# Four attention layers on one core: the row fills split in halves and moved, and two of six operand copies issued by GpSimd

## Chip, cores and metric

The kernel runs on one core of a Trainium2 chip. The metric is the device time of one execution in microseconds; where several runs are given it is their median. Engines are named TensorE (PE), VectorE (DVE), ScalarE (ACT), GpSimd (POOL) and SyncE (SP). PEld is the weight load of TensorE, which runs beside its matmuls.

## The reference, cut to what matters

Sixteen sequences `x` of 128 tokens and 128 channels pass through four layers with a context of the same shape. Layer L3 has a self and a cross attention, so there are five attention parts. A part does, for each sequence:

```python
# L0: layernorm of both inputs, 8 heads of 16 channels; all others 16 heads of 8 channels
q, k, v = x @ Wq + bq, ctx @ Wk + bk, ctx @ Wv + bv      # L3 self: all three from x
scores = einsum('bhqd,bhkd->bhqk', q, k) / sqrt(d)        # L1: causal and padding mask; L3 self: the same
probs = softmax(scores)
x = x + einsum('bhqk,bhkd->bhqd', probs, v)               # L2, L3: also @ Wo + bo
# L2: then x += gelu(x @ W1 + b1) @ W2 + b2
# L3 self: layernorm; L3 cross: layernorm, the same kind of MLP, layernorm
```

Everything is float32 in and out.

## The kernel before, in words

The 16 sequences are taken in 8 sets of two. A *unit* is one set in one of the five parts (L0, L1, L2, L3S, L3C), so there are 40 units, numbered `u` = 8 x part + set. `SETS` is 8, `RING` is 4.

**The split.** Scores are made by bf16 matmuls whose contraction rows carry the float32 product in pieces. For a unit, TensorE projects q and k (`qk`, L978 and L979), ScalarE adds the bias into `qk_f32` (L642), then ScalarE writes the first bf16 term (`split`, L654, signal `split1_done`). For units from 2 on GpSimd makes the remainder (`rest`, L560), the second term (`term1`, L562, `split2_done`) and the third (`term2`, L568, `split_done`). For units 0 and 1 VectorE does this (L777, L780, L785).

**The stacks.** The list `PRODUCTS` has six pairs of terms, (0,0), (0,1), (1,0), (1,1), (0,2), (2,0). For each one DMA (`stack` step `c` = 0 to 5, L442) spreads the two terms from the 128 channel partitions into rows of an operand tile, one row per channel of a head and 16 heads (8 in L0) side by side: 128 KB in pieces of 512 bytes. The tile is `pairs8` in L0 and one half (64 rows) of `pairs16` later: units `u` and `u+4` share it. All six are issued by SP. Stacks 4 and 5 use the third term, so SP waits for `split_done` before stack 4; before stack 0 it waits until the last attention matmul of unit `u-4` has read the tile. The readers of the stacks are the first score matmul of the unit on TensorE (L930, through `stacked`), and ScalarE's `split` of unit `u+2`, which overwrites the terms that the stacks read.

**The rows behind the stacks.** Below its 48 product rows a half of `pairs16` has 4 mask rows and 3 rows for the negated maxima. They start as constants: `fill_rows(pool, r)` (L385) copies 7 rows of `template` to 16 heads of half `r`, 112 KB. The sources and the targets are seven partitions. Halves 0 and 1 are filled ahead of GpSimd's steps, 2 and 3 at its step `ln_in` of unit 0. `mask_rows` (L397) then writes a unit's mask rows, 32 KB. L0 has its own tiles, whose 3 rows ScalarE fills at the start (L610).

**Softmax.** VectorE takes the maxima of the scores (L823), splits them (`nmax`, L833, L836), TensorE transposes them (`n_tr`, L995), VectorE copies them (L839), and SP writes them with a DMA into the tile (L458). Then TensorE makes the scores a second time, transposed and with the maxima taken off (`attn`, L1016), ScalarE exponentiates them (L703), TensorE multiplies with v (`pv`, L1043). From L1 on the scores of unit `u+1` run interleaved with the attention matmuls of unit `u`.

**The order.** It is fixed ahead: `schedule()` gives every step a position of 8 per unit (`PREPARE`, `STACK_AT`, `SCORE_AT`, `CHAIN`, `LAST`) and sorts them into `STEPS`. Each of the five engines walks the same list and does its own part of each step, in order, so a wait on an engine holds up all its later steps. The order of some steps around the change, as the list gives it (numbers are units, the dots stack numbers):

```
L0  ln_in 0, ln_in 1, ln_in 2, stack 0.4, 0.5, qk 1, ln_in 3, score 0, qk 2, stack 1.4, 1.5, rest 2
L0  term2 5, ln_in 7, mask 0, stack 5.4, 5.5, rest 6, term1 6, term2 6, mask 1, stack 6.4, 6.5, rest 7
L1  rest 15, term1 15, term2 15, rest 16, term1 16, term2 16, stack 15.4, 15.5, qk 17
L2  rest 17, term1 17, stack 16.4, term2 17, stack 16.5, qk 18, rest 18, term1 18, stack 17.4, term2 18, stack 17.5
L3C rest 33, stack 32.4, term1 33, term2 33, stack 32.5
```

GpSimd has more at some of these steps: `ln_in` makes the reciprocal deviations (L531, L534), at unit 2 four small loads (L547 to L550), at unit 4 a weight load; `mask` makes the mask rows of L1 (L495, L498) and, for units 0 to 3, writes them (L397) after waiting for all four fills; `term2` has a weight load (L577) in L1 and L2, and mask rows (L397) for units 12 to 19, 24 to 27 and 32 to 35. SP issues the loads of `x_tok` and `c_tok` for all sets first (L407, L409).

Of the kernel before, what the change touches and what calls it, by code (L numbers as in the profile page):

```python
# [50 lines left out]
MISC_BANKS = 3  # L51
SLOT = 8
SPLIT_BY_DVE = 2
EPS_LN, EPS_LAST = 1e-5, 1e-6
# [161 lines left out]
def build(nc, x, ctx_in, weights, cols, rows, valid, valid_t, pad, pad_t, out):  # L216
    with ExitStack() as stack:
# [3 lines left out]
        def sem(name):  # L221
            return stack.enter_context(nc.semaphore(name))
# [67 lines left out]
        tokens_landed = [sem(f"tokens_landed{s}") for s in range(SETS)]  # L290
        stack_landed = [sem(f"stack_landed{r}") for r in range(RING)]
        max_landed = [sem(f"max_landed{r}") for r in range(4)]
        out_landed = sem("out_landed")
# [10 lines left out]
        mask_landed = [sem(f"mask_landed{r}") for r in range(RING)]  # L304
        fill16_landed = sem("fill16_landed")
        misc_ready = sem("misc_ready")
# [66 lines left out]
        def stacked(eng, u):  # L373

            eng.wait_ge(stack_landed[u % RING], (u // RING + 1) * 16 * len(PRODUCTS))

# [3 lines left out]

        def fill_rows(pool, r):

            first = product_rows(SETS)
            rows_ = slice(HALF * (r % 2) + first, HALF * (r % 2) + first + MASK_ROWS + TERMS)
            pool.dma_start(pairs16[r // 2][rows_, :, :, :].rearrange("p h a n -> p h (a n)"),  # L385
                           template[first:first + MASK_ROWS + TERMS, :, :, :].rearrange("p a b n -> p (a b n)")
                           .unsqueeze(1).to_broadcast([MASK_ROWS + TERMS, 16, 2 * TOK])).then_inc(fill16_landed, 16)

        def mask_rows(pool, u):

            part = u // SETS
            tile, base = stack_of(u)
            source = {L1: mask_rows_l1[:, PAIR * (u % SETS):PAIR * (u % SETS + 1), :],
                      L2: zero_rows[:, :].rearrange("p (b n) -> p b n", b=PAIR),
                      L3S: mask_rows_l3s[:, :, :], L3C: mask_rows_l3c[:, :, :]}[part]
            first_row = base + product_rows(u)
            pool.dma_start(tile[first_row:first_row + MASK_ROWS, :, 1, :],  # L397
                         source.rearrange("p b n -> p (b n)").unsqueeze(1)
                         .to_broadcast([MASK_ROWS, HEADS[part], TOK])).then_inc(mask_landed[u % RING], 16)

        block = stack.enter_context(nc.Block())

        @block.sync
        def _(sp):
# [10 lines left out]
            for step in STEPS:  # L415
                u = step.u
                part = u // SETS
                heads = HEADS[part]
                if step.kind == "stack":

                    c = step.b
                    tile, base = stack_of(u)

                    if c == 0:
                        sp.wait_ge(split1_done, u + 1)
                    if c == 1:
                        sp.wait_ge(split2_done, u + 1)
                    if c == 4:
                        sp.wait_ge(split_done, u + 1)
                    if c == 0:  # L430
                        if u >= RING and (u - RING) // SETS >= min(part, L1):

                            freed = the("attn", u - RING, PAIR - 1, heads // QUAD - 1)
                            sp.wait_ge(attn_ready, NUM[freed] + 1)
                        if u == SETS:
                            sp.wait_ge(fill16_landed, 16 * RING)
                    d = D // heads
                    tq, tk = PRODUCTS[c]
                    terms = terms_ring[u % 2]
                    gap = TERMS + tk - tq  # L440

                    sp.dma_start(tile[base + c:base + product_rows(u):len(PRODUCTS), :, :, :],  # L442
                                 terms[:, :, :, :].rearrange("p a t n -> p (a t) n")[:, tq:tq + gap + 1:gap, :])\
                        .then_inc(stack_landed[u % RING], 16)
                if step.kind == "store":
# [17 lines left out]
        def _(pool):  # L463
# [19 lines left out]
            pool.wait_ge(rows_ready, 3)  # L483
            fill_rows(pool, 0)
            fill_rows(pool, 1)
            for step in STEPS:
# [15 lines left out]
                if step.kind == "mask" and u < RING:  # L502

                    pool.wait_ge(fill16_landed, 16 * RING)
                    pool.wait_ge(mask_l1_ready, u + 1)
# [30 lines left out]
                if step.kind == "ln_in" and u == 0:  # L536
                    fill_rows(pool, 2)
                    fill_rows(pool, 3)
                    pool.memset(causal_t[:, :], 0.0).then_inc(negated_diagonal, 1)
# [24 lines left out]
                if step.kind == "term2" and u >= SPLIT_BY_DVE:  # L564
                    pool.wait_ge(split2_done, u + 1)
                    if 2 <= u < SETS:
                        pool.wait_ge(maxterms_ready, ub(the("nmax", u - 2, 1)) + 1)
                    pool.tensor_tensor(terms[:, :, 2, :], rest[:, :, :], terms[:, :, 1, :], ALU.subtract)\  # L568
                        .then_inc(split_done, 1)
                if step.kind == "term2" and part in W_EACH:  # L570

# [6 lines left out]
                if step.kind == "term2" and u in MASKED_ANEW and u >= SETS + RING:  # L578
# [5 lines left out]
                    if u == L3S * SETS:  # L584
                        pool.wait_ge(mask_l3_ready, 1)
                    mask_rows(pool, u)
                if step.kind == "square":
                    half = slice(2 * step.b, 2 * step.b + 2)
# [551 lines left out]
```

## Time and profile before

| | us |
|---|---|
| runs of the kernel | 496.58, 497.14, 505.9 |
| median | 497.14 |
| profiled execution, its own time | 495.54 |
| its span, first to last instruction | 493.8 |

The span is 1.74 us shorter than the execution's own time; that rest lies around the instructions. All times from the trace count from the start of the span. The page's busy shares are averages; the chain of waits follows the work that ended last back to its releasers.

### The profile page before, as it was taken

The page shows a single profiled execution, that of the slowest core. Times are in us where ns is not written, and L with a number is a line of the kernel's source. Part 1 is how long each engine was busy: PE and PEld are TensorE (multiplying, and loading weights), DVE is VectorE, ACT ScalarE, POOL GpSimd, SP SyncE. Part 2 cuts the span into 40 slices and gives each one's busy share as a digit, 9 for nine tenths or more (in the row PEclk, how much of TensorE's full clock was granted, in tenths as well). Part 3 has the DMA queues.
Part 4 walks back from the last instruction along what each step waited for, and adds up shares of the span by engine and source line. Part 5 has one row for each costly group of instructions (what it writes and reads, how often), then busy time and mean ns, then how long its engine had stood idle before and what let it go on. Part 6 is the DMA issues. An engine that isn't in the chain of part 4 may idle for free.

```text
span 493.8 us, 17187 instructions
## 1 busy us (share of the span) xinstructions
PE 447.9 (91%) x6720; PEld 302.8 (61%) x6720; DVE 386.2 (78%) x1099; ACT 321.9 (65%) x660; POOL 234.2 (47%) x290
## 2 busy tenths in 40 slices
PE   3478989899999998899999999999999999999981
PEld 2365656556666665577767666666666666666761
DVE  6587897778878878889988877888889987877552
ACT  2345765457676667678777676667677787777841
POOL 6246576856734534454554444334444543222345
PEclk9657998899999999999999999999999999999997
DMA  7644343643433444433433322222244341220001
GB/s 125 167 101 104 91 102 82 142 115 87 106 84 93 111 110 98 101 93 94 91 77 62 68 51 68 68 69 69 53 86 94 76 93 47 63 56 14 14 23 32
DMA packets 71579, 40.48 MB, mean 82 GB/s; under 512 B 7896, under 2 KB 70584, under 8 KB 71500
## 3 DMA queue, kind: packets, MB, share of 16 engines
q1 hardware_dynamic: 69280, 36.04, 30.2%
q0 software_dynamic: 2112, 3.24, 4.7%
q8 instruction: 55, 0.90, 0.8%
q14 instruction: 24, 0.20, 0.1%
q10 hardware_dynamic: 108, 0.10, 0.1%
HBM read 4.74 MB, written 1.05 MB: 12 GB/s over the span
## 4 chain that ended last, share of the span: by engine, by line
PE 76%; DVE 10%; DMA 4%; issue 3%; ACT 2%; POOL 2%; SPq 1%; POOLq 0%; DVEq 0%; ACTq 0%
PE attn_ps L1016 17%; PE o_ps L1043 15%; PE misc_ps L1073 6%; PE misc_ps L1064 5%; PE misc_ps L978 5%; PE misc_ps L1050 4%; PE score_ps L897 4%; PE misc_ps L984 3%; PE misc_ps L979 3%; DVE max_words L823 3%; PE misc_ps L1056 2%; DVE normed_in L759 2%; PE misc_ps L995 2%; DMA c_tok<-in_ctx_dram 2%; PE score_ps L930 2%
## 5 line engine op out<-in xcount | busy, mean ns | idle before, releaser
L823 DVE TENSOR_REDUCE max_words<-score_ps 128x4 f32<-128x512 f32 x288 | 193.7, 683 | 50.5 <-PE score_ps L930 47.6
L703 ACT ACTIVATE probs<-attn_ps 128x512 f32<-128x512 f32 x288 | 169.7, 601 | 74.4 <-PE attn_ps L1016 68.5
L1016 PE MATMUL attn_ps<-pairs 55*128 55x128 bf16 (+1 forms) x1152 | 113.7, 220 | 9.0 <-DMA pairs<-max_rows 3.4
L930 PE MATMUL score_ps<-pairs 52*128 52x128 bf16 (+1 forms) x1152 | 115.4, 222 | 2.3 <-DMA pairs<-terms 2.0
L560 POOL TENSOR_TENSOR rest<-qk_f,terms 128x512 f32<-128x512 f32 x38 | 44.2, 1162 | 114.2 <-ACT terms L654 114.2
L1016 PEld LDWEIGHTS attn_ps<-pairs 55*128 55x128 bf16 (+1 forms) x1152 | 64.9, 95 | 53.3 <-issue 26.8
L1043 PE MATMUL o_ps<-probs,v 128*32 128x128 f32 x2304 | 96.8, 281 | 0.1
L930 PEld LDWEIGHTS score_ps<-pairs 52*128 52x128 bf16 (+1 forms) x1152 | 67.3, 96 | 6.5 <-DMA pairs<-terms 2.8
L1043 PEld LDWEIGHTS o_ps<-probs,v 128*32 128x32 f32 x2304 | 53.5, 109 | 23.4 <-issue 9.5
L568 POOL TENSOR_TENSOR terms<-rest,terms 128x512 bf16<-128x512 f32 x38 | 44.0, 1158 | 9.7 <-DVE max_words L836 7.2
L712 ACT ACTIVATE o_sb<-o_ps 128x256 f32<-128x256 f32 x80 | 30.9, 386 | 23.7 <-PE o_ps L1043 22.7
L531 POOL TENSOR_SCALAR var_eps<-mean_var 128x2 f32<-128x2 f32 (+1 forms) x32 | 7.1, 222 | 81.1 <-DVE mean_var L744 80.8
L562 POOL TENSOR_TENSOR terms<-qk_f,terms 128x512 bf16<-128x512 f32 x38 | 43.9, 1154 | 0.0
L1050 PE MATMUL misc_ps<-ident,o_sb 128*128 128x128 f32 x160 | 35.0, 302 | 1.2 <-DVE attn_tok L859 1.2
L1073 PE MATMUL misc_ps<-hidden,w 128*128 128x256 f32 x128 | 33.3, 388 | 1.7 <-ACT hidden L691 1.6
L1064 PE MATMUL misc_ps<-xT,w 128*128 128x256 f32 x128 | 31.2, 386 | 0.3 <-DVE xT L881 0.3
L865 DVE SCALAR_TENSOR_TENSOR xT<-misc_ps,col,xT 128x256 f32<-128x256 f32 x40 | 19.0, 480 | 11.5 <-PE misc_ps L1073 6.6
L590 POOL TENSOR_TENSOR gelu_arg<-half_h 128x512 f32<-128x512 f32 x16 | 16.2, 1030 | 23.1 <-ACT half_h L688 23.1
L1073 PEld LDWEIGHTS misc_ps<-hidden,w 128*128 128x128 f32 x128 | 23.0, 190 | 6.4 <-ACT hidden L691 2.0
L534 POOL TENSOR_TENSOR rstd<-var_eps,minus_half 128x2 f32<-128x2 f32 (+1 forms) x32 | 25.6, 799 | 2.7
L654 ACT ACTIVATE terms<-qk_f 128x512 bf16<-128x512 f32 x40 | 25.3, 632 | 2.3 <-DMA pairs<-terms 1.7
L1064 PEld LDWEIGHTS misc_ps<-xT,w 128*128 128x128 f32 x128 | 23.0, 190 | 4.0 <-issue 0.8
(121 smaller groups left out, 751.0 us busy)
## 6 DMA issues: line engine op xcount, KB each, us to landing
pairs<-terms SPq DMA_DIRECT2D x240, 128.0 KB
x_tok<-in_x_dram SPq DMA_DIRECT2D x8, 128.0 KB, 2.6
c_tok<-in_ctx_dram SPq DMA_DIRECT2D x8, 128.0 KB, 3.0
pairs<-max_rows SPq DMA_DIRECT2D x64, 12.0 KB
w<-in_weights_dram POOLq DMA_DIRECT2D x8, 128.0 KB, 3.2
out_dram<-x_tok SPq DMA_DIRECT2D x8, 128.0 KB, 1.8
w<-in_weights_dram POOLq DMA_DIRECT2D x5, 192.0 KB, 3.3
pairs<-template POOLq DMA_DIRECT2D x4, 112.0 KB, 7.9
```

Source lines behind the costliest of these rows:

```text
L560: pool.tensor_tensor(rest[:, :, :], qk_f32[:, :, :], terms[:, :, 0, :], ALU.subtract)
L562: pool.tensor_tensor(terms[:, :, 1, :], qk_f32[:, :, :], terms[:, :, 0, :], ALU.subtract)\
L568: pool.tensor_tensor(terms[:, :, 2, :], rest[:, :, :], terms[:, :, 1, :], ALU.subtract)\
L703: act.activation(probs[n % PROBS_RING][:, :, :].rearrange("p h q -> p (h q)"), attn_ps[n % 2][:, :], ACT.Exp, scale=float(D // HEADS[part] ...
L712: act.activation(o_sb[n % 2][:, :], o_ps[:, 0:2 * P], ACT.Copy)\
L823: dve.tensor_reduce(max_words[ub(step) % 2][:, QUAD * g:QUAD * (g + 1)], score_ps[n % 2][:, :].rearrange("p (h k) -> p h k", h=QUAD), AX_X ...
L930: return pe.matmul(score_ps[NUM[step] % 2][:, j * S:(j + 1) * S], tile[score_rows(u), QUAD * g + j, 0, b * S:(b + 1) * S], tile[score_rows ...
L1016: last = pe.matmul(attn_ps[n % 2][:, j * S:(j + 1) * S], pairs[attn_rows(u), h, 1, b * S:(b + 1) * S], pairs[attn_rows(u), h, 0, b * S:(b ...
L1043: last = pe.matmul(o_ps[32 * j:32 * j + 32, region * P:(region + 1) * P], values, probs[n % PROBS_RING][:, j, :], start=part == L0 or g % ...
L1050: last = pe.transpose(bank[:, k * P:(k + 1) * P], o_sb[ub(step) % 2][:, k * P:(k + 1) * P], ident[:, :])
L1064: last = pe.matmul(bank[:, half * TOK:(half + 1) * TOK], weight(f"w1_{part}_{2 * b + half}"), xT[s][:, :], start=True, stop=True)
L1073: last = pe.matmul(bank[:, 0:TOK], weight(f"w2_{part}_{c}"), hidden[:, c, :], start=(c == 0), stop=(c == 3))
```

## The change

Three things are edited. `BY_POOL` is 4. The stacks with `c` of 4 and 5 are issued by GpSimd at the same places of the list, with a ring of signals of their own (`late_landed`); GpSimd waits before stack 4 for `split_done` of the unit and for the last attention matmul of unit `u-4`. SP keeps stacks 0 to 3 and their waits. The four fills become eight halves of 8 heads each (56 KB), and are issued by GpSimd right after `rest` and after `term2` of units 2 to 5, half `r` of `pairs16` at unit `r + 2`; their signal becomes one per half, and the mask step of unit `u` waits for its own half alone.

```diff
+BY_POOL = 4
+        late_landed = [sem(f"late_landed{r}") for r in range(RING)]
-        fill16_landed = sem("fill16_landed")
+        fill16_landed = [sem(f"fill16_landed{r}") for r in range(RING)]
         def stacked(eng, u):
-            eng.wait_ge(stack_landed[u % RING], (u // RING + 1) * 16 * len(PRODUCTS))
+            eng.wait_ge(stack_landed[u % RING], (u // RING + 1) * 16 * BY_POOL)
+            eng.wait_ge(late_landed[u % RING], (u // RING + 1) * 16 * (len(PRODUCTS) - BY_POOL))
-        def fill_rows(pool, r):
+        def fill_rows(pool, r, heads):
-            pool.dma_start(pairs16[r // 2][rows_, :, :, :].rearrange("p h a n -> p h (a n)"),
+            pool.dma_start(pairs16[r // 2][rows_, heads, :, :].rearrange("p h a n -> p h (a n)"),
...
-                           .unsqueeze(1).to_broadcast([MASK_ROWS + TERMS, 16, 2 * TOK])).then_inc(fill16_landed, 16)
+                           .unsqueeze(1).to_broadcast([MASK_ROWS + TERMS, 8, 2 * TOK])).then_inc(fill16_landed[r], 16)
+        def stack_rows(eng, u, c):
+            tile, base = stack_of(u)
+            tq, tk = PRODUCTS[c]
+            gap = TERMS + tk - tq
+            eng.dma_start(tile[base + c:base + product_rows(u):len(PRODUCTS), :, :, :],
+                          terms_ring[u % 2][:, :, :, :].rearrange("p a t n -> p (a t) n")[:, tq:tq + gap + 1:gap, :])\
+                .then_inc((stack_landed if c < BY_POOL else late_landed)[u % RING], 16)
...
-                if step.kind == "stack":
+                if step.kind == "stack" and step.b < BY_POOL:
...
-                    if c == 4:
-                        sp.wait_ge(split_done, u + 1)
...
-                        if u == SETS:
-                            sp.wait_ge(fill16_landed, 16 * RING)
...
+                    stack_rows(sp, u, c)
...
-            fill_rows(pool, 0)
-            fill_rows(pool, 1)
...
-                    pool.wait_ge(fill16_landed, 16 * RING)
+                    pool.wait_ge(fill16_landed[u], 32)
...
-                    fill_rows(pool, 2)
-                    fill_rows(pool, 3)
...
+                if step.kind in ("rest", "term2") and SPLIT_BY_DVE <= u < SPLIT_BY_DVE + RING:
+                    if u == SPLIT_BY_DVE:
+                        pool.wait_ge(rows_ready, 3)
+                    fill_rows(pool, u - SPLIT_BY_DVE, slice(0, 8) if step.kind == "rest" else slice(8, 16))
...
+                if step.kind == "stack" and step.b >= BY_POOL:
+                    if step.b == BY_POOL:
+                        pool.wait_ge(split_done, u + 1)
+                        if u >= RING and (u - RING) // SETS >= min(part, L1):
+                            freed = the("attn", u - RING, PAIR - 1, HEADS[part] // QUAD - 1)
+                            pool.wait_ge(attn_ready, NUM[freed] + 1)
+                    stack_rows(pool, u, step.b)
```

## Rows read from the trace of the kernel before

**Rows 1.** The page: busy time, and the span in 40 slices.

```profile
PE 447.9 (91%) x6720; PEld 302.8 (61%) x6720; DVE 386.2 (78%) x1099; ACT 321.9 (65%) x660; POOL 234.2 (47%) x290
...
PE   3478989899999998899999999999999999999981
```

**Rows 2.** Chain that ended last, to 70 us (start us, us, what).

```profile
3.74 11.50 DMA c_tok<-in_ctx_dram
...
32.03 2.81 DVE normed_in L759 x4
```

**Rows 3.** Timeline of the first 33 us (start us, us, engine line, tiles, idle before).

```profile
3.85 1.51 POOL L385 DMA_DIRECT2D pairs<-template  x2 [0.31 <-POOL template L480]
...
5.08 5.03 SPq L409 DMA_DIRECT2D c_tok<-in_ctx_dram  x1
...
15.26 0.49 DVE L740 BATCH_NORM_STATS2 stats<-x_tok 128x6 f32<-128x128 f32 x2 [4.51 <-DMA c_tok<-in_ctx_dram]
...
24.14 0.67 POOL L547 DMA_DIRECT2D validt_raw<-in_valid_t_dram  x1
24.22 0.61 DVE L759 TENSOR_SCALAR normed_in<-x_tok,mean_var,rstd 128x128 f32<-128x128 f32 x2 [1.47 <-POOL rstd L534]
...
28.08 0.61 PE L930 MATMUL score_ps<-pairs 96*128 96x128 bf16 x4 [0.66 <-DMA pairs<-terms]
...
32.17 1.21 POOL L560 TENSOR_TENSOR rest<-qk_f,terms 128x512 f32<-128x512 f32 x1 [0.19 <-ACT terms L654]
```

**Rows 4.** Windows: stretch, us, busy of PE, PEld, DVE, ACT, POOL, PE clock, DMA share, GB/s.

```profile
4.00:8.00 4.00, 1.03 (x4) 0.63 (x4) 2.47 (x13) 1.94 (x3) 3.69 (x6) 1.00 0.97 209
8.00:13.00 5.00, 3.47 (x11) 2.75 (x12) 2.40 (x8) 1.29 (x3) 1.12 (x5) 1.00 0.83 51
17.00:21.00 4.00, 1.08 (x4) 0.71 (x4) 2.85 (x9) 0.58 (x2) 1.00 (x1) 0.53 0.68 196
```

**Rows 5.** Issues of stacks and fills (ns min/median/max); then landing of L577, 155 to 200 us.

```profile
L442 SPq DMA_DIRECT2D pairs<-terms x240: 565/623/1970, 21.2 to 433.1; - x120
L385 POOL DMA_DIRECT2D pairs<-template x4: 618/661/861, 3.9 to 7.6; - x4
...
DMA to landing us min/median/max: 2.9/3.7/4.6
```

**Rows 6.** Landing of GpSimd's mask rows, L397, 155 to 200 us.

```profile
DMA to landing us min/median/max: 3.3/4.1/4.5
```

**Rows 7.** Timelines of POOL, SP and PE, 67 to 100 us.

```profile
67.09 1.09 POOL L495 TENSOR_SCALAR mask_rows_l<-valid_raw 4x256 bf16<-4x256 uint8 x1
67.42 2.68 SPq L442 DMA_DIRECT2D pairs<-terms  x4
70.38 1.16 POOL L560 TENSOR_TENSOR rest<-qk_f,terms 128x512 f32<-128x512 f32 x1
73.72 0.39 PE L930 MATMUL score_ps<-pairs 96*128 96x128 bf16 x4
...
85.96 1.17 POOL L560 TENSOR_TENSOR rest<-qk_f,terms 128x512 f32<-128x512 f32 x1
...
93.12 1.17 POOL L560 TENSOR_TENSOR rest<-qk_f,terms 128x512 f32<-128x512 f32 x1
```

**Rows 8.** Timelines of ACT and POOL, splits of units 17 to 20.

```profile
167.57 0.66 ACT L654 ACTIVATE terms<-qk_f 128x512 bf16<-128x512 f32 x1
...
168.31 1.15 POOL L560 TENSOR_TENSOR rest<-qk_f,terms 128x512 f32<-128x512 f32 x1 [4.95 <-ACT terms L654]
...
172.34 0.64 POOL L397 DMA_DIRECT2D pairs<-zero_rows  x1
...
177.41 0.66 ACT L654 ACTIVATE terms<-qk_f 128x512 bf16<-128x512 f32 x1
...
186.97 0.66 ACT L654 ACTIVATE terms<-qk_f 128x512 bf16<-128x512 f32 x1
...
196.04 0.62 ACT L654 ACTIVATE terms<-qk_f 128x512 bf16<-128x512 f32 x1
```

More of the change, by code:

```diff
@@ L418, in _ @@
                 heads = HEADS[part]
-                if step.kind == "stack":
+                if step.kind == "stack" and step.b < BY_POOL:
                     c = step.b
-                    tile, base = stack_of(u)
                     if c == 0:
@@ L434, in _ @@
                             sp.wait_ge(attn_ready, NUM[freed] + 1)
-                        if u == SETS:
-                            sp.wait_ge(fill16_landed, 16 * RING)
[L437 to L444, printed above, removed]
+                    stack_rows(sp, u, c)
                 if step.kind == "store":
```

## The prediction

> **What bounds the kernel now.** I read the page's busy times and slices first. TensorE is busy 447.9 of 493.8 us, and its slices are 8 or 9 tenths full from the fourth on, but 3, 4 and 7 in the first three [rows 1]. So in the middle an edit off TensorE pays nothing unless it makes TensorE wait, and a delay comes out one to one; at the start there are idle stretches to win. The chain of waits, read next for the start, shows one large item: from 3.74 on, 11.50 us go to the landing of the context tokens of set 1 [rows 2]. The timeline shows why that transfer is slow. GpSimd issues the first two fills at 3.85, and SP, busy with the token loads, is then held 5.03 us in one issue [rows 3]. In 4 to 8 us the DMA engines are 97% busy at 209 GB/s; in 8 to 13 us still 83%, but only 51 GB/s move; in 17 to 21 us, without fills, 196 GB/s at 68% [rows 4]. Engines that are busy and move little are waiting on something narrow. The fills read seven partitions and write seven, so I put the slow stretch down to them. Their replacement in time is what the change is about.
>
> After that I looked for where stacks decide, since two of six change their queue: the score of unit 0 waits for a stack landing, 0.66 us [rows 3]; and ScalarE's split of unit u+2 needs all stacks of unit u landed.
>
> **Part one: the fills leave the start.** VectorE idled 4.51 us before the statistics of set 1, for that landing [rows 3]. Without fills the tokens should land before VectorE is free, at 15.26 - 4.51 = 10.75 us. So the statistics, and the reciprocal deviations and normalising behind them, come 4.5 us earlier: that is the most this edit alone gives. What is late next is the score of unit 0. It needs stacks 4 and 5, which GpSimd now issues after `ln_in` of set 2 and the four small loads behind it. Those loads start at 24.14 and the last at 26.00 for 0.55 [rows 3]; moved by 4.5 they end at 22.05. Two issues of 0.65 follow, the second from 22.7. With a landing of 3.5 (an estimate, between the 2.9 and 3.7 of [rows 5]) it is there at 26.2. The score ran at 28.08, so there only 1.9 us are left of the 4.5. Then a side effect: VectorE's four `normed_in` of set 3 took 2.81 [rows 2], beside `rest` and `term1` of unit 2 on GpSimd from 32.17; two of them without such company took 0.61, so four 1.1 or a little more [rows 3]. Set 3's deviations come early while `rest` waits for the score, so the two separate: 1.7 more. Value taken: 1.9 + 1.7 = 3.6 gained. Ends: 1.9, and 4.5 + 1.7 = 6.2.
>
> A rule of the Trainium skill bears on the overlap: the page "Advanced Engine Details and Errata" says that the second VectorE port is shared with GpSimd, whose instructions and VectorE's two-port ones block each other. The 2.81 agrees. By "DMA: Bandwidth & Descriptors", section "SWDGE vs HWDGE vs iDMA", it would also hold GpSimd's descriptor writing, and so speak against the stacks' new place. Here the rows show no such price: the small load at 24.14 beside `normed_in` at 24.22 took 0.67, the last one 0.55 [rows 3].
>
> **Part two: the eight halves beside sets 2 to 5.** A fill's issue takes GpSimd 0.62 to 0.86, median 0.66 [rows 5]; a half has half the pieces, so I take 0.65. Eight are 5.2 us of GpSimd for 2.7 before. GpSimd is in front of nothing there except `term1` and the deviations, and in this stretch the chain goes through VectorE; cost taken, zero. Their 448 KB can hold up stacks as they held up tokens, but now in eight portions: zero to 2 us, taken 0, since the chain to 70 us has no stack landing on it in what I kept of it and each half is an eighth of the traffic.
>
> **Part three: 80 stack issues move from SP to GpSimd.** SP's issue takes 0.62 in the median [rows 5]; GpSimd's own issues of 32 to 128 KB take 0.55 to 0.86 [rows 3, 5]. No row shows GpSimd issuing 256 pieces of 512 bytes. Nearest in size is the 128 KB load; I take 0.65, and 1.3 (twice that) as the upper end; below 0.55 nothing speaks for it. Taking 1.25 us per unit from SP gives nothing where SP waits anyway; bounded from above by 1 us in all, taken 0.
>
> Where is GpSimd itself in front? Two places.
>
> (a) 67 to 100 us. From 85.96 to 93.12 it goes round without a gap in 7.16 us [rows 7], and two issues make that 8.5. First, unit 5: SP issued its last four stacks from 67.42 in 2.68, the last one at about 69.4, and the score ran at 73.72. GpSimd must finish mask step 0 first (from 67.09; `rest` of unit 6 followed at 70.38). With one fill before it, 0.65, and the first stack before the second, 0.65, the last is issued at 71.7, 2.3 later. The same landing and 73.72 make the score 2 us late, less what the last SP stack gains by a shorter queue. For units 6 to 9 GpSimd's lag grows by 1.3 each, but the units' spacing of 8 to 9 us takes that up. Taken: 1.5 lost. Ends: 0 and 3.
>
> (b) The entry to L2, units 15 to 19. Stack 5 of unit u now leaves behind `term2` of u+1, its weight load and its mask rows; split u+2 waits for its landing; and `rest` of u+2 waits for that split. That is a circle that the kernel before doesn't have. Its length by the rows: split 17 starts at 167.57, GpSimd's last item starts at 172.34 for 0.64, so 5.41; plus stack 4 inserted, 0.65: stack 5 is issued 6.06 after the split [rows 8]. Landing: 2.9 to 4.6 for a weight load, 3.3 to 4.5 for mask rows with a median of 4.1 [rows 5, 6]. With 4.1 the circle is 10.16. The splits stood 9.84, 9.56 and 9.07 apart [rows 8], so it is late by 0.32 + 0.60 + 1.09 = 2.0; unit 15, whose two stacks also leave behind unit 16, adds an estimated 0.5. From unit 20 on mask rows are missing and periods are longer. Taken: 2.5 lost, out of TensorE, which has no slack to give back. Ends: landing 2.9 makes 8.96, no loss; 4.6 makes 10.66, and 0.82 + 1.10 + 1.59 + 1.0 = 4.5.
>
> By the Trainium skill, "DMA: Bandwidth & Descriptors", section "Anatomy of one DMA — SWDGE (gpsimd) path", a GpSimd DMA takes about 2.0 us plus bytes over 436 GB/s, 2.3 for a stack. Then the circle would be 8.4 and (b) cost nothing, and the sum below would be 2.5 lower. GpSimd's DMAs here took 2.9 at the least [rows 5], so I go by the rows.
>
> In L3C stack 5 has the same place, behind `term2` of u+1 and mask rows. Before, it was the last of six from SP and equally late; taken 0, up to 1.
>
> **The sum.** -3.6 + 0 + 1.5 + 2.5 + 0 = +0.4 on the profiled execution of 495.54, so 495.9. That execution lay 1.6 under the median of the runs, 497.14, so the median to expect is 497.5.
>
> **The rivals.**
> - *The start alone counts.* The stacks land within 3.5 us and GpSimd's lag in 67 to 100 us is absorbed, so (a) and (b) are 0 or a small rest. For it: units lie 9 us apart and GpSimd is busy 234.2 of 493.8. Against it: the gapless stretch of [rows 7]. Price: -3.6 to -4.5, median 493.
> - *GpSimd's issue of a 256-piece stack is the price* (slower). Each takes 1.3 us where 0.65 is taken. The circle becomes 11.5: late by 1.6 + 1.9 + 2.4 + 1.8 (unit 15) and some 0.4 more at unit 19, 8.1 instead of 2.5; stretch (a) loses 2.6 more, and L3C's four such units about 3. Sum 0.4 + 5.6 + 2.6 + 3 = 11.6: median 509. It decides from an issue of about 0.8 on, where (b) outweighs the start. For it: no row has this form. Against it: 112 pieces take 0.66 and four small ones no less than 0.55.
> - *The fills were not what held the tokens.* The start stays full through ScalarE's L0 fills and the broadcast loads, and the landing still comes near 15. Part one is then 0: median 501. For it: 97% busy before the fills can have moved much. Against it: 51 GB/s after those loads are through.
>
> **How the numbers follow.** Forecast 0.48, start alone 0.27, dear issue 0.13, fills innocent 0.12. All ends favourable give 495.54 - 6.2 + 1.6 = 491; the forecast with all bounds against it (-1.9 + 3 + 4.5 + 2) gives 504.7, cut to 503 to leave out about one in ten above, most of it the dear issue. Range 491.5 to 503. A difference of 2%, 9.9 us, is about what a measurement of this kernel tells from no change. Faster by more than that needs more than the whole start's gain: 0.03. Slower by more needs the dear issue at nearly its full price or a stack of costs: 0.09. Within: 0.88.
>
> **What would show it.** Right: no landing over 5 us for tokens of set 1, statistics of set 1 near 10.8, no SP issue of several us; score 0 near 26; GpSimd issues of stacks near 0.65; splits 17 to 20 about 10.2 apart with ScalarE idle before them on a stack's landing. Wrong: GpSimd issues above 0.8 or landings above 5; `pairs` fills with landings that stop score matmuls in 30 to 70 us; splits spaced as before; a start as slow as now.

## Result and profile after the change

The changed kernel ran at 514.51 us, median of 4 runs (509.82 to 518.75). The kernel before ran at 496.58 to 506.92 beside it, and the ratio is 1.0332 with a 95% interval of 1.028 to 1.0384: slower by more than 2%. The forecast was 497.5, in a range of 491.5 to 503. The runs of the kernel before lie in two groups about 11 us apart, and the ratios compare with the lower one. The profiled execution of after took 509.82, the shortest of its four, with a span of 508.0, against 495.54 and 493.8 before. The *granted clock* of the windows below is TensorE's clock as a share of 2.4 GHz; at any moment it is 1.00 or 0.50, and a value between is the average of a stretch.

The page of after, the lines that answer to [rows 1], with the clock and the chain:

```profile
PE 451.8 (89%) x6720; PEld 303.8 (60%) x6720; DVE 398.1 (78%) x1099; ACT 321.8 (63%) x660; POOL 294.0 (58%) x374
...
PE   3559879798999999899999999999999999999981
...
PEclk9967999976999989999999999999999999999997
...
PE 60%; DVE 21%; DMA 8%; issue 4%; POOL 3%; ACT 2%; SPq 0%; POOLq 0%; DVEq 0%; ACTq 0%
```

GpSimd is busy 60 us longer, and VectorE 12 us longer though it does the same work. TensorE's slices are still 8 and 9 tenths full but for two of 7, and the two slices from 102 to 127 us have clock 7 and 6. VectorE holds 21% of the chain instead of 10%.

The start, timeline of after, answering to [rows 3] (start, length, engine, line, tiles, idle before):

```profile
10.62 0.29 DVE L749 BATCH_NORM_STATS2 stats<-x_tok 128x6 f32<-128x128 f32 x1
...
21.97 1.25 POOL L409 DMA_DIRECT2D pairs<-terms  x2
...
26.93 0.59 PE L939 MATMUL score_ps<-pairs 96*128 96x128 bf16 x4 [5.03 <-DMA pairs<-terms]
...
30.81 1.46 DVE L768 TENSOR_SCALAR normed_in<-x_tok,mean_var,rstd 128x128 f32<-128x128 f32 x2
31.04 1.15 POOL L555 TENSOR_TENSOR rest<-qk_f,terms 128x512 f32<-128x512 f32 x1 [3.36 <-ACT terms L663]
...
32.19 2.11 DVE L768 TENSOR_SCALAR normed_in<-c_tok,mean_var,rstd 128x128 f32<-128x128 f32 x2
```

The statistics of set 1 stand at 10.62, and the windows of the stretch that had moved 51 GB/s [rows 4] now read:

```profile
4.00:8.00 4.00, 1.09 (x4) 0.72 (x4) 2.40 (x13) 1.94 (x3) 2.10 (x6) 1.00 0.83 229
8.00:13.00 5.00, 3.57 (x11) 2.84 (x12) 3.44 (x16) 1.39 (x3) 0.99 (x3) 1.00 1.08 236
```

So the fills were what held the tokens. But the score of unit 0 gained only 1.15 us, since TensorE now waits 5.03 us for GpSimd's stacks: the second is issued at 22.55 and lands 4.25 us later. The four `normed_in` of set 3 take 3.57 us, not 2.81: they still lie beside `rest`, and the first fill half follows there.

The stacks that GpSimd issues, from the view of line L409 over the whole span (length in ns, then issue to landing):

```profile
L409 POOL DMA_DIRECT2D pairs<-terms x80: 588/810/952, 22.0 to 447.1; - x80
...
DMA to landing us min/median/max: 2.4/3.8/5.6
```

The entry to L2, ScalarE's splits of units 15 to 20 and one turn of GpSimd, answering to [rows 8]; then TensorE's first matmul for the scores of unit 15:

```profile
157.41 0.64 ACT L663 ACTIVATE terms<-qk_f 128x512 bf16<-128x512 f32 x1
167.50 0.66 ACT L663 ACTIVATE terms<-qk_f 128x512 bf16<-128x512 f32 x1
178.38 0.63 ACT L663 ACTIVATE terms<-qk_f 128x512 bf16<-128x512 f32 x1 [1.08 <-issue]
189.90 0.66 ACT L663 ACTIVATE terms<-qk_f 128x512 bf16<-128x512 f32 x1
199.42 0.64 ACT L663 ACTIVATE terms<-qk_f 128x512 bf16<-128x512 f32 x1
208.70 0.63 ACT L663 ACTIVATE terms<-qk_f 128x512 bf16<-128x512 f32 x1 [0.23 <-DMA pairs<-terms]
```

```profile
190.64 1.16 POOL L555 TENSOR_TENSOR rest<-qk_f,terms 128x512 f32<-128x512 f32 x1 [5.53 <-ACT terms L663]
...
195.90 0.78 POOL L409 DMA_DIRECT2D pairs<-terms  x1
...
178.55 0.23 PE L906 MATMUL score_ps<-causal_s,ident_bf 32*32 32x128 bf16 x4 [1.37 <-DMA pairs<-terms]
```

The splits stand 10.1, 10.9, 11.5, 9.5 and 9.3 apart. Stack 5 is issued 195.90 - 189.90 = 6.00 us after its split: the forecast had 6.06. Stack 5 of units 15 to 18 landed at 178.30, 189.54, 199.35 and 208.63, each 0.07 to 0.36 us before the split that waits for it: splits 17 to 20 follow that landing. It took 4.7 and 5.2 us for units 15 and 16, and 3.5 and 3.3 for 17 and 18: that is why the spacing falls from 11.5 to 9.5.

The stretch from 105 to 125 us was not in the forecast at all. Windows of after (stretch, us, busy of PE, PEld, DVE, ACT, POOL, clock, DMA share, GB/s), then the timeline:

```profile
100.00:105.00 5.00, 4.70 (x64) 2.99 (x65) 3.05 (x9) 2.85 (x6) 4.71 (x7) 1.00 0.55 140
105.00:110.00 5.00, 4.33 (x55) 2.58 (x54) 4.14 (x11) 1.58 (x3) 4.70 (x6) 0.85 0.38 102
110.00:115.00 5.00, 4.49 (x38) 2.53 (x38) 2.86 (x5) 1.95 (x4) 3.22 (x5) 0.50 0.68 137
115.00:120.00 5.00, 4.00 (x59) 2.04 (x59) 3.36 (x7) 1.70 (x4) 4.64 (x6) 0.50 0.28 78
120.00:125.00 5.00, 5.00 (x90) 3.29 (x88) 3.35 (x10) 2.17 (x4) 0.89 (x2) 0.78 0.21 53
```

```profile
105.38 1.34 POOL L557 TENSOR_TENSOR terms<-qk_f,terms 128x512 bf16<-128x512 f32 x1
105.51 1.26 DVE L842 TENSOR_TENSOR max_words<-max_words 128x16 f32<-128x16 f32 x1
106.06 0.39 PE L939 MATMUL score_ps<-pairs 52*128 52x128 bf16 x4
...
107.12 0.22 PE L1004 MATMUL misc_ps<-ident_bf,max_words 128*48 128x128 bf16 x1 [0.67 <-DVE max_words L845]
...
109.25 0.60 PE L939 MATMUL score_ps<-pairs 52*128 52x128 bf16 x4
...
114.77 1.08 DVE L845 TENSOR_TENSOR max_words<-max_words 128x16 f32<-128x16 f32 x1
...
116.00 0.27 PE L1004 MATMUL misc_ps<-ident_bf,max_words 128*48 128x128 bf16 x1 [1.51 <-DVE max_words L845]
```

VectorE's small subtraction at 105.51 takes 1.26 us beside GpSimd's `term1`; its median is 0.17. TensorE waits for it. At 108.5 the granted clock goes to 0.50 (1.2 GHz) for 13.7 us, and four score matmuls take 0.60 instead of 0.39. Before, the clock read 1.00 in 100 to 130 us. That the late maxima made the clock fall is not shown; two runs below speak against it as the only cause.

The slow subtractions are on the chain that ended last. Between 70 us and the fall of the clock it holds four of them in after, and two in before (start us, us, what):

```profile
71.01 2.49 DVE max_words L842
...
88.82 1.76 DVE max_words L842
...
98.12 1.25 DVE max_words L842
...
105.51 1.27 DVE max_words L842
```

```profile
71.38 1.31 DVE max_words L833
...
93.16 2.28 DVE max_words L833
```

That is 6.8 us against 3.6: 3.2 us more that VectorE lost on the chain, before the long stretch at half clock.

To see where the 14.2 us of span went I took the first score matmul of each unit from the timelines. Changed kernel minus kernel before: -1.1 us at unit 0, +0.1 at unit 2, +0.9 at unit 5, +1.3 at unit 8, +8.0 at unit 10, +9.6 at unit 14, +11.8 at unit 20, +12.2 at unit 31, +14.0 at unit 36, +14.2 at the end. So 1.3 came up to unit 8, 6.7 in units 8 and 9, 1.6 to unit 14, 2.2 in the L2 entry, 1.8 in L3C.

### The profile page after: what moved, and what is told of

It reads as the page before. It is cut to its first block, busy times and chain, and to the rows that moved or that the text cites. A ratio compares the mean times of both kernels' runs of the same rounds, so it can differ in the third digit from the quotient of the medians.

```text
span 508.0 us, 17242 instructions
## 1 busy us (share of the span) xinstructions
PE 451.8 (89%) x6720; PEld 303.8 (60%) x6720; DVE 398.1 (78%) x1099; ACT 321.8 (63%) x660; POOL 294.0 (58%) x374
## 3 DMA queue, kind: packets, MB, share of 16 engines
q1 hardware_dynamic: 53152, 25.55, 21.8%
## 4 chain that ended last, share of the span: by engine, by line
PE 60%; DVE 21%; DMA 8%; issue 4%; POOL 3%; ACT 2%; SPq 0%; POOLq 0%; DVEq 0%; ACTq 0%
PE attn_ps L1025 13%; PE o_ps L1052 11%; DVE max_words L832 7%; PE misc_ps L1082 6%; DMA pairs<-max_rows 5%; PE misc_ps L1073 5%; PE misc_ps L987 4%; PE score_ps L906 3%; PE misc_ps L1059 3%; DVE normed_in L768 3%; DMA pairs<-terms 3%; DVE max_words L842 3%; PE misc_ps L988 3%; PE misc_ps L993 2%; PE misc_ps L1065 2%
## 5 line engine op out<-in xcount | busy, mean ns | idle before, releaser
L1025 PE MATMUL attn_ps<-pairs 55*128 55x128 bf16 (+1 forms) x1152 | 114.9, 222 | 8.8 <-DMA pairs<-max_rows 4.8
L1052 PEld LDWEIGHTS o_ps<-probs,v 128*32 128x32 f32 x2304 | 53.9, 110 | 23.7 <-issue 10.1
L409 POOL DMA_DIRECT2D pairs<-terms x80 | 60.1, 799 | 1.1 <-POOL terms L563 0.9
L563 POOL TENSOR_TENSOR terms<-rest,terms 128x512 bf16<-128x512 f32 x38 | 45.6, 1199 | 8.8 <-DVE max_words L845 6.8
L557 POOL TENSOR_TENSOR terms<-qk_f,terms 128x512 bf16<-128x512 f32 x38 | 46.4, 1221 | 0.1
L651 ACT ACTIVATE qk_f<-misc_ps,col 128x256 f32<-128x256 f32 x24 | 11.3, 472 | 26.9 <-PE misc_ps L988 21.7
L874 DVE SCALAR_TENSOR_TENSOR xT<-misc_ps,col,xT 128x256 f32<-128x256 f32 x40 | 19.0, 479 | 11.5 <-PE misc_ps L1082 6.6
L842 DVE TENSOR_TENSOR max_words<-max_words 128x16 f32<-128x16 f32 (+1 forms) x80 | 25.3, 316 | 2.7
```

The source lines that it names most:

```text
L409: eng.dma_start(tile[base + c:base + product_rows(u):len(PRODUCTS), :, :, :], terms_ring[u % 2][:, :, :, :].rearrange("p a t n -> p (a t) ...
L557: pool.tensor_tensor(terms[:, :, 1, :], qk_f32[:, :, :], terms[:, :, 0, :], ALU.subtract)\
L1025: last = pe.matmul(attn_ps[n % 2][:, j * S:(j + 1) * S], pairs[attn_rows(u), h, 1, b * S:(b + 1) * S], pairs[attn_rows(u), h, 0, b * S:(b ...
L1052: last = pe.matmul(o_ps[32 * j:32 * j + 32, region * P:(region + 1) * P], values, probs[n % PROBS_RING][:, j, :], start=part == L0 or g % ...
```

## Experiments

Medians are over 4 or 6 runs. Beside them the kernel before ran 29 times: 494.53 to 509.32, median 503.8, mean 501.7. "At unit n" is always the start of that unit's scores in the profiled execution against the kernel before.

**Fills alone.** The fills as changed, all six stacks issued by SyncE as before.

```diff
-                if step.kind == "stack" and step.b < BY_POOL:
+                if step.kind == "stack":
...
-                if step.kind == "stack" and step.b >= BY_POOL:
...
-                    stack_rows(pool, u, step.b)
```

> All six stacks stay with SP; only the fills move, in halves, beside sets 2 to 5. Theory A (the stacks' new place on GpSimd costs, the fills gain): score 0 near 24 us, the first set of L1 2 to 4 us earlier than before, time 2 to 4 us under before. Theory B (fills beside the sets hold stacks and maxima up, so the loss is theirs): the gain of the start is gone by 70 us and the time is 3 us or more above before.

Measured: 504.21 (502.26 to 507.79), ratio 1.0164 (1.0115 to 1.0214). Unit 0 starts 6.3 us early and unit 5 4.5 us early; unit 8 2.0 early, unit 9 2.8 late, unit 10 6.6 late, and 7.9 remain to the end. Its windows show where:

```profile
80.00:90.00 10.00, 10.00 (x80) 6.21 (x76) 5.49 (x16) 4.36 (x9) 6.41 (x8) 0.50 0.49 110
90.00:100.00 10.00, 8.61 (x112) 5.41 (x109) 6.89 (x20) 5.31 (x11) 7.18 (x8) 1.00 0.45 111
100.00:110.00 10.00, 10.00 (x82) 6.20 (x80) 5.38 (x15) 2.47 (x5) 3.74 (x5) 0.52 0.35 91
110.00:120.00 10.00, 8.52 (x106) 4.63 (x108) 6.89 (x15) 4.24 (x8) 5.42 (x6) 0.50 0.26 68
```

The start's gain is real, 4.5 us once nothing waits for GpSimd's stacks. It is lost again in stretches at half clock: in 100 to 110 us TensorE ran 82 matmuls, and in the kernel before 143. VectorE was not slower here than before (the first of its two subtractions took 17.7 us for all 80, before 18.2), so the clock falls without the changed kernel's load on GpSimd too.

**Stacks alone.** The fills where they were before, stacks 4 and 5 by GpSimd.

```diff
-                if step.kind in ("rest", "term2") and SPLIT_BY_DVE <= u < SPLIT_BY_DVE + RING:
...
+            fill_rows(pool, 0)
+            fill_rows(pool, 1)
```

> Fills stay at the start; stacks 4 and 5 are GpSimd's. Theory A: the whole loss of the changed kernel and the start's 1 us on top, so 12 to 17 us above before, with units 8 to 10 and 15 to 18 spaced wider. Theory B: within 3 us of before.

Measured: 522.91 (519.65 to 527.6), ratio 1.0514 (1.0474 to 1.0554): 2.7 us late at unit 0, 6.7 at unit 8, 16.1 at unit 10, 24.7 at unit 20, 27.5 at unit 36. The new queue is the costly part, and the fills' part takes some of it back.

**Stacks right behind the third term.** The changed kernel, with both GpSimd stacks issued directly after `term2` of their own unit.

```diff
+                if (step.kind == "term2" and u >= SPLIT_BY_DVE) or (step.kind == "stack" and step.b == BY_POOL
+                                                                   and u < SPLIT_BY_DVE):
+                    pool.wait_ge(split_done, u + 1)
...
+                    for c in range(BY_POOL, len(PRODUCTS)):
+                        stack_rows(pool, u, c)
```

> The changed kernel, with stacks 4 and 5 issued by GpSimd right behind term2 of their own unit (from unit 2 on), ahead of weight load, mask rows and the next unit's rest: as many issues and as much traffic, other places. If the place in GpSimd's order is the price (circle with unit u+1): units 15 to 19 spaced as before, L3C too, and 3 to 5 us of the 14 come back. If issue time or traffic is the price: within 2 us of the changed kernel. The stretch of 85 to 128 us, where GpSimd has no gap, should stay slow by both.

Measured: 520.88 (518.84 to 524.15), ratio 1.0491 (1.0438 to 1.0544). A miss: units 14 and 15 together took 20.5 us instead of 22.3, and L3C from unit 31 to 36 lost 0.6 instead of 1.8, but 8.3 us were lost by unit 5, another 10.3 in units 8 and 9, partly at half clock, and 6.0 between units 20 and 31. In the first stretch both stacks stand ahead of the next set's reciprocal deviations on GpSimd; what costs so much there, and in the last, was not followed. Relief in one place came with a greater loss in the crowded one.

**Small issues.** The kernel before, with two added 2 KB copies to an unused tile on GpSimd at the places of stacks 4 and 5; nothing waits for them but GpSimd itself.

```diff
+                if step.kind == "stack" and step.b >= 4:
...
+                    pool.dma_start(scratch[2 * (u % RING) + step.b - 4][:, :], zero_rows[:, :])\
+                        .then_inc(small_landed[u % RING], 16)
```

> The kernel before (all stacks by SP, fills at the start) with two more GpSimd DMAs of 2 KB per unit to scratch, at the places and with the waits where the change issues stacks 4 and 5. They cost GpSimd's time and move nothing; nobody waits for them but their own ring. If GpSimd's time (about 1.3 us a unit) is the price in 67 to 128 us: that stretch loses most of what it lost with the change, 5 to 9 us in all. If the traffic in the other queue or the late landing is the price: within 2 us of before. The loss of units 15 to 18 should be absent, since no stack hangs on GpSimd.

Measured: 507.9 (505.49 to 508.94), ratio 1.0215 (1.0178 to 1.0252). An issue took 0.54 us in the median. The units are late by 2.2 us at unit 5, 4.5 at units 9 and 10, 4.6 at unit 20, 6.2 at unit 36, with no half clock in units 8 and 9, but 9.5 us of it in units 5 to 7 where the kernel before had 6.8. Another 6.5 us lie behind the last instruction of GpSimd's list (10.2 us to the end of the span, 3.7 before), a cost of this kernel alone: the changed one has 3.9 there. So 43 us of issues on GpSimd, with the waits ahead of them, cost about 6 us of span in this execution with no operand behind them. Time on GpSimd's list is a price in itself, most of it before unit 10.

**TensorE kept working.** Three kernels with two added matmuls of 128 columns (their result is not used) ahead of TensorE's waits for the maxima in units 4 to 9, and for operands in units 4 to 7, where two waits also change their order: in the changed kernel, in the kernel before, and in the one with the fills alone.

```diff
+            def filler(u, bank, last=9):
+                if 4 <= u <= last:
+                    for _ in range(2):
+                        pe.matmul(bank[:, 3 * P:4 * P], ident[:, :], ident[:, :], start=True, stop=True,
...
+                    filler(u, bank)
                     pe.wait_ge(maxterms_ready, m + 1)
```

> The changed kernel with idle work for TensorE: for units 4 to 9 two more float32 matmuls of 128 columns ahead of each wait for the maxima (transpose and, in L0, attention) and, in L0, for the stacks; their results are overwritten. If the granted clock at half rate in units 8 and 9 is what costs the 6.7 us there, and TensorE's waits before it are what make it fall: the clock stays at its upper level from unit 5 to 10, units 8 and 9 take under 21 us together for 26.4, and the time falls by 3 to 6 us although work is added. If GpSimd's lag is the price there: the clock may differ, the time does not fall.

> The kernel before with the same idle work. Its runs lie in two groups some 11 us apart. If the clock in units 8 and 9 makes the two groups: all runs lie in the lower one, 494 to 500. If not: two groups as before.

> Only the fills moved, stacks by SP, with the idle work for TensorE. If the start's gain of 4.4 us was lost to the clock alone: 490 to 495 us, under every run of the kernel before. If not: above 500, as without the idle work.

Measured: changed 515.77 (512.25 to 521.6), before 508.83 (503.88 to 516.46), fills alone 502.95 (498.3 to 510.98). The filler costs more than it saves in two of the three kernels, and the runs stay about as far apart as without it. But the three profiled executions have full clock from 54 us to the tail, one line each (changed, before, fills alone):

```profile
54.00:130.00 76.00, 70.08 (x887) 50.02 (x879) 55.88 (x158) 39.83 (x85) 58.23 (x71) 1.00 0.43 96
```

```profile
54.00:130.00 76.00, 71.91 (x935) 51.35 (x933) 54.83 (x163) 40.69 (x86) 46.74 (x52) 1.00 0.39 94
```

```profile
54.00:130.00 76.00, 73.41 (x1009) 52.34 (x1011) 56.05 (x158) 41.60 (x87) 50.35 (x59) 1.00 0.41 98
```

That makes them a comparison without the clock. Starts of units (us):

```
unit                        0     2     5     8    10    14    20    31    36   span
before, filler           28.7  46.0  74.5 105.3 127.6 166.4 225.3 360.9 409.7  502.1
fills alone, filler      22.6  42.2  70.6  99.4 121.8 160.6 219.5 354.4 403.8  496.6
changed, filler          27.0  45.6  76.6 107.5 130.2 171.2 231.0 367.0 417.9  510.5
fills' part (2nd - 1st)  -6.1  -3.8  -3.9  -5.9  -5.8  -5.8  -5.8  -6.5  -5.9   -5.5
stacks' part (3rd - 2nd) +4.4  +3.4  +6.0  +8.1  +8.4 +10.6 +11.5 +12.6 +14.1  +13.9
```

With filler and at full clock the fills bring 5.5 us and the stacks' new queue costs 13.9; together +8.4. The medians of the six runs each give -5.9 and +12.8.

The other 5.8 of the changed kernel's 14.2 are clock only if the filler costs each kernel the same, and it does not: it fills waits. In units 8 and 9 all three kernels take 22.4 to 22.8 us. Without filler, the kernel before takes 19.7 there, and the changed kernel's instructions take 21.8 in an execution whose clock stayed full (the one with the L2 entry by SyncE, below, which is the changed kernel up to unit 13). The changed kernel itself took 26.4, so 4.6 of its 6.7 there are clock and 2.1 are not. By unit 14 the two executions stand 2.7 us apart. Together the runs put the clock's part at 3 to 6 us of the 14.2 and the rest, 8 to 11, at GpSimd's new work less the fills' gain.

**Units 0 and 1 by SyncE.** The changed kernel, stacks 4 and 5 of the first two units issued by SyncE.

```diff
-                if step.kind == "stack" and step.b < BY_POOL:
+                if step.kind == "stack" and (step.b < BY_POOL or u < SPLIT_BY_DVE):
```

> The changed kernel, but SP issues stacks 4 and 5 of units 0 and 1. If the late stack of unit 0 (behind GpSimd's four small loads) is what gave the start's gain back: score 0 near 22 us and sets 2 to 4 about 4 us earlier than in the changed kernel, as with the fills alone. If it is the fills beside the sets: no change at sets 2 to 4. Whether the 4 us reach the end is open, since the clock decides in between.

Measured: 511.62 (502.81 to 516.59), ratio 1.0165 (1.006 to 1.027). Unit 0 starts 5.5 us early, as fits a start held by GpSimd's stacks; at unit 5 it is +0.2 and at unit 10 +12.6, with half clock in 86 to 96 us and in 110 to 127. What is won at unit 0 is gone by unit 5, and units 14 to 19 cost 4.2, partly at half clock, and L3C 2.1.

**L2 entry by SyncE.** The changed kernel, stacks 4 and 5 of units 14 to 19 by SyncE.

```diff
+BY_SP = range(14, 20)
...
+                if step.kind == "stack" and (step.b < BY_POOL or u in BY_SP):
```

> The changed kernel, but stacks 4 and 5 of units 14 to 19 are issued by SyncE, as before the change; all else is changed. Circle theory: the six splits from unit 15 to 20 go back to the spacing of before (9.3 to 9.9 us instead of 9.3 to 11.5) and the time falls by 2.5 to 4 us, to about 511. Clock theory: what GpSimd's work does to VectorE and through it to TensorE's clock is the whole loss; then undoing six units gives 0 to 1 us, and units 9 and 10 stay as slow as in the changed kernel.

Measured: 508.48 (503.25 to 514.63), ratio 1.0175 (1.0128 to 1.0222), 6 us less than the changed kernel. Its splits of units 15 to 20:

```profile
154.93 0.64 ACT L669 ACTIVATE terms<-qk_f 128x512 bf16<-128x512 f32 x1
164.79 0.66 ACT L669 ACTIVATE terms<-qk_f 128x512 bf16<-128x512 f32 x1
174.44 0.66 ACT L669 ACTIVATE terms<-qk_f 128x512 bf16<-128x512 f32 x1
184.28 0.66 ACT L669 ACTIVATE terms<-qk_f 128x512 bf16<-128x512 f32 x1
193.78 0.66 ACT L669 ACTIVATE terms<-qk_f 128x512 bf16<-128x512 f32 x1
202.98 0.62 ACT L669 ACTIVATE terms<-qk_f 128x512 bf16<-128x512 f32 x1
```

They are 9.9, 9.7, 9.8, 9.5 and 9.2 apart. From unit 14 to 20 it loses nothing (+6.9 to +6.5) where the changed kernel loses 2.2. That is the circle, near the forecast's size. Its profiled execution also has no half clock in units 8 and 9 (+3.7 at unit 8, +4.6 at unit 9, +5.8 at unit 10), so the rest of the 6 us need not be the edit's. VectorE's slow subtractions are all there (24.0 us for 80, up to 2.48), so they do not by themselves make the clock fall.

**Units 0 to 9 by SyncE.** The same switch with another range.

```diff
+BY_SP = range(10)
```

> The changed kernel, but stacks 4 and 5 of units 0 to 9 are issued by SyncE: up to unit 9 it is the kernel with the fills moved alone, behind it the changed one. Theory that GpSimd's issues in the crowded stretch (67 to 110 us) are the greater part of the ten us between the kernel with the fills moved alone and the changed one: the time falls by 5 to 8 us, to 507 to 509. Circle theory: it falls by what units 5 to 9 lost to the later issue, 1.5 us, with another 4 from the start, of which units 8 to 10 take most back by half clock: 0 to 3 us in all, and the spacing of splits 15 to 20 stays at 9.3 to 11.5 us.

Measured: 509.41, four runs of 499.25, 507.44, 511.39 and 515.59; no interval could be given. Its profiled execution is the 499.25, and it shows the case without the fall of the clock:

```profile
80.00:90.00 10.00, 7.80 (x104) 4.95 (x96) 9.01 (x17) 5.35 (x11) 8.97 (x10) 1.00 0.52 121
90.00:100.00 10.00, 8.14 (x104) 5.16 (x104) 7.00 (x24) 4.36 (x9) 7.21 (x10) 1.00 0.45 113
100.00:110.00 10.00, 9.47 (x163) 5.89 (x160) 8.18 (x24) 5.68 (x11) 7.34 (x9) 1.00 0.56 131
```

Until its first stack by GpSimd, at 101.7 us, this is the kernel with the fills alone, instruction by instruction. Here unit 9 starts 4.5 us early; there it started 2.8 us late. The two executions ran on different chips; in their rows they differ by the granted clock, and that is the likely cause of the 7.3 us. Behind unit 9 this kernel loses 4.4 us up to unit 14 (from -4.5 to -0.1), with 3.4 us of half clock in it and the first GpSimd stacks; what costs that was not followed. Then it goes to +1.3 at unit 20 and +3.4 at unit 36: circle and L3C again.

**One stack by GpSimd.** `BY_POOL = 5`: stack 4 goes back to SyncE.

```diff
-BY_POOL = 4
+BY_POOL = 5
```

> The changed kernel with BY_POOL = 5: stack 4 is issued by SyncE and only stack 5 by GpSimd. Halves the issue work that GpSimd gets (40 issues of about 0.8 us less). If the price goes by GpSimd's issue time, the circle is 0.8 us shorter and gives back 2 to 3 us, and the 67 to 100 us stretch another 1 us: 510 to 512. If it goes by having any stack behind GpSimd's order of work and a landing of about 4 us, the circle stays near its 10.8 us and the time stays at 513 to 515.

Measured: 511.03 (504.36 to 516.05), ratio 1.0235 (1.0104 to 1.0367). From unit 10 to 20 the lateness goes from 11.9 to 12.6 only: with one issue less between split and stack 5 the circle is short enough, and splits 15 to 18 stand 9.9, 10.2 and 10.1 apart. L3C still loses 1.8. Units 9 and 10 start 5.8 and 11.9 us late, more than the 4.3 and 8.0 of the changed kernel, at half clock from 102 to 130 us. The issue of its stack 5, of 256 pieces like the others, took 0.62 us in the median (0.54 to 0.69).

**A small filler.** The fills alone, with one matmul ahead of the wait for maxima in units 6 to 8.

```diff
+                if 6 <= u <= 8:
+                    pe.matmul(bank[:, 3 * P:4 * P], ident[:, :], ident[:, :], start=True, stop=True,
```

> The fills moved, all stacks issued by SyncE, and one 128-column filler matmul (result not used) ahead of TensorE's wait for each unit's maxima in units 6, 7 and 8 alone. A candidate to beat both kernels: the start's gain of 4 to 5 us is kept if a little work is enough to hold the clock in units 7 to 10, which gives 492 to 496 in the lower group of runs. If units 7 to 10 lose it whatever TensorE does in its waits, the time stays at the 504 of the fills moved alone; if the little filler does not hold the clock, the granted clock is half in a stretch between 80 and 120 us, as there.

Measured: 507.66 (503.44 to 509.05), ratio 1.0233 (1.0156 to 1.031), half clock in 82 to 92, 102 to 116 and 119 to 129 us of the profiled execution. So little does not hold the clock. No version beat the kernel before.

## Why the prediction was wrong, point by point

The sum by stretches, changed kernel minus kernel before (us). The third column is from the profiled executions; the last is from those with filler, at full clock, where waits are partly hidden.

| stretch | forecast | measured | with filler |
|---|---|---|---|
| start, to unit 3 | -3.6 | -0.4 | +0.9 |
| (a) units 3 to 9 | +1.5 | +8.4 | +1.8 |
| units 10 to 13 | 0 | +1.6 | +2.1 |
| (b) L2 entry, units 14 to 19 | +2.5 | +2.2 | +0.9 |
| units 20 to 30 | 0 | +0.4 | +0.4 |
| L3C and the end | 0 | +2.0 | +2.3 |
| sum | +0.4 | +14.2 | +8.4 |

- **What bounds the kernel, and that delays come out one to one:** right, with one omission. TensorE's clock can be at its lower level for part of an execution, and then the same work takes longer.
- **The fills held the tokens:** right. Statistics of set 1 at 10.62 (forecast 10.75), 236 GB/s where 51 had been. The rival that the fills were innocent falls.
- **The start, -3.6:** failed. The score of unit 0 came at 26.9, forecast 26.2, since the stack landed in 4.25 and not in 3.5. The second 1.7, from set 3's `normed_in` parting from GpSimd's work, failed: they took 3.57, beside `rest` at 31.04 and a fill half. At unit 2 nothing was left (+0.1). I had counted 1.9 as kept, although units 0 and 1 each pass over GpSimd's stacks. With these stacks on SyncE 3.3 to 4.1 were left at unit 2.
- **Eight halves, 0:** no engine waited for their landing in the changed kernel or with the fills alone, and the latter still has its 4.5 at unit 5.
- **The issue, 0.65:** mis-sized. It measured 0.59 to 0.95, mean 0.80: the point that the forecast named for the dear issue to decide. As neighbouring issues overlap, the 80 occupy GpSimd for 60.1 us, 0.75 each. The landing, 4.1 taken, measured 3.8 in the median, 5.2 at most in the L2 entry and 5.6 at most in all, so two of the forecast's signs of being wrong showed. By the Trainium skill, "DMA: Bandwidth & Descriptors", section "Anatomy of one DMA — SWDGE (gpsimd) path", it would be 2.3 for a stack, an estimate; the fastest of 80 took 2.4, so here that figure is near the floor and not the usual case.
- **(a) 67 to 100 us, +1.5:** this is the step that failed most, +8.4 from unit 3 to 10. I had let GpSimd's lag be taken up by the spacing of the units. It was not: up to unit 8 it was +1.7, near the forecast, and units 8 and 9 cost 6.7 more. GpSimd's tensor operations fell on VectorE's subtractions of the maxima, which are on the chain (6.8 us of them before the clock fell, 3.6 before the change); I had used the slowing of VectorE by GpSimd for the start alone. And 13.7 us at half clock followed, a term that the sum did not have. The +1.8 with filler hides waits and is too low: in the execution with the L2 entry by SyncE it is +4.6, of which 2.1 in units 8 and 9 at full clock (units 5 to 7 have 2.3 us more of half clock than before the change). GpSimd's round of 7.16 us in [rows 7] was also not without a gap: it was busy for 6.16 of it.
- **(b) the L2 entry, +2.5:** right in mechanism and of the right order. Measured +2.2 from unit 14 to 20, +3.3 to unit 17 with some half clock in unit 15; at full clock +1.9 to unit 17, of which 1.0 came back by unit 20. With units 0 to 9 by SyncE, at full clock from unit 14 to 20, it is +1.4. It is gone when those six units are undone. The circle took 10.9, 11.5, 9.5 and 9.3, forecast 10.16 each time, with 6.00 to issue, forecast 6.06.
- **L3C, 0 with an end of 1:** mis-sized, 1.8 from unit 31 to 36 in the changed kernel and 1.6 to 2.1 in the five others that keep both stacks at these places. It stays 1.8 with stack 4 back on SyncE and is 0.6 with both right behind their own `term2`, so it is the place of stack 5, behind `term2` of the next unit, that costs.
- **Units 10 to 13, 0:** a stretch that the sum passed over. It cost 1.6, and 2.1 with filler, there 1.5 of it a wait for the landing of `max_rows`.
- **The rivals:** the dear issue was closest in time (509), but its mechanism holds in part only. The issue cost 0.80, not 1.3, and the circle lost 2.2, not 8.1. That it comes near is luck: it has neither the slowed VectorE nor the clock. All bounds against the forecast gave 504.7, 9.8 below the measured time; what they lacked is in stretch (a), units 10 to 13 and L3C.

What is left open: why the clock falls in one run and not in another of the same code. Over all 97 runs with a granted clock on record I took the time at half clock as twice the missing share of the span. The 14 runs of the kernel before under 500 us have 26 us of it on average, the 15 above have 53. Within one kernel the time rises by 0.3 us for each such microsecond. The changed kernel has 57 on average, and its mean time lies 7.5 us above the mean of those 15 runs, near the +8.4 from above. With the fills alone it is 51, and none of its 6 runs was under 502. That the moved parts make the fall likelier is what these counts suggest. By what it was not shown: no kernel held the clock in all its runs.

## What to carry to other kernels

Before handing DMA issues to an engine with idle time, ask what its work does to others while it runs. GpSimd had 53% idle, and 60 us of issues cost about 14 us, part of it by slowing VectorE. Follow a moved issue round: if the engine that issues it also waits for what its landing frees, that is a circle, and its length against the spacing of the loop gives the order of the loss (2.5 forecast, 0.9 to 2.2 measured). Compare two executions only after reading their granted clock, and take a mechanism's size from executions at equal clock. Work added to hold the clock hides waits, so it makes such a difference too small.

## What was unexpected of the hardware

- A VectorE subtraction on 128x16 elements, 0.17 us in the median, took up to 2.48 us in the changed kernel and up to 2.27 before; the 80 of L842 took 25.3 us instead of 18.2 in all. Counting both subtractions, 13 took over 0.5 us in the changed kernel and 5 before, and each of these 18 ended 0.02 to 0.05 us behind the end of a GpSimd tensor operation: VectorE's operation got done only when GpSimd's was through. The Trainium skill, "Advanced Engine Details and Errata", section "GPSIMD Details", says that GpSimd shares a read and a write interface with VectorE and conflicts with VectorE instructions that have two SBUF inputs. This subtraction has two, and the rows agree.
- Issuing a DMA on GpSimd took 0.54 us for four pieces and 0.62 for 256 where stack 5 went alone, so the number of pieces hardly matters. With both stacks, stack 4 took 0.91 in the median and stack 5 0.77. Stack 4 reads two terms that lie five places apart and stack 5 two neighbours; whether that decides was not tested.
- 80 added small copies on GpSimd lengthened the end of the program by 6.5 us; 80 larger ones in the place of SyncE's did not.
- Time at half clock depends on the run: the same instructions brought unit 9 4.5 us early once and 2.8 us late the other time.
